# Graph attention on one core: steps of two edge slots instead of three, the carried sum taken by TensorE and copied back by ScalarE

## The chip, the cores and the metric

The kernel runs on 1 core of a Trainium2 chip. The metric is the device time in microseconds (us). The kernel before took 4021.01 us, the median of 3 runs (4016.24 to 4050.6). The profiled execution took 4017.71 us; its span in the trace is 4015.6 us.

## The reference, cut to what matters

There are 12500 nodes of 256 features, 8 heads of 32, and 200000 edges between random nodes. All is fp32.

```
q, k, v = (h @ W.T + b).reshape(N, 32, 8)       # for Wq, Wk, Wv; q * 32**-0.5
s = einsum('edh,edh->eh', q[row], k[col])       # one score per edge and head
e = exp(s - segment_max(s, row)[row])
attn = e / segment_sum(e, row)[row]
out = segment_sum(attn * v[col], row)
return layernorm(x + out @ Wo.T + bo)
```

## The kernel before, in words

A first part sorts the edges by node, counts the edges of every node (a histogram), orders the nodes by that count, and writes a table `kv_rows` to HBM with one row per node: its keys (256) and, for each head, its 32 values and a 1 (8 x 33 = 264). The 12500 nodes are cut into 98 tiles of 128, so that a partition holds one node, and nodes with nearly the same number of edges share a tile. A last part (`finish`) divides by the sum of weights, multiplies by Wo and normalises.

Between the two stands `one_round`, the main loop. A slot is one edge for each of the 128 nodes of a tile, and a tile has as many slots as its fullest node has edges. A step takes G = 3 slots of one tile. The number of steps, 598, is fixed when the program is built, as an upper bound. With these inputs, the sum over the tiles of the fullest node's edges divided by 3 and rounded up is 559; the other 39 steps are padding, which gather row 0 of the table for every slot and work on a 99th tile that nobody reads. For steps of two slots the same count gives 813 of 849, and 36 of padding. No node has more than 36 edges, so that one round of `C` slots is enough.

What a step does, with its engines and lines:

- ScalarE copies the step's node numbers into `idx` (`indices`, L973; it looks the place up in a table, by a register load).
- GpSimd starts one indirect DMA for each slot (`gather`, L931): 128 rows of 520 numbers into `kv`. SyncE loads the tile's 128 rows of q (`load_q`, L952). Both run up to U = 6 steps ahead.
- VectorE multiplies keys by q (`score`, L790), sums each head (`score_sum`, L797), looks tile and place of a later step up (`look_up`, L853), copies the tile's old maximum behind the scores (L802), adds the mask (L805), takes the new maximum (L812) and subtracts it (`differences`, L818).
- ScalarE takes exp of the differences (`weights`, L977), that of the old maximum too, which is the factor by which the old sum has to shrink.
- VectorE multiplies the values of the first G - 1 slots by their weights (`weigh`, L825), ScalarE those of the last slot, head by head, in 8 instructions (`weigh_last`, L987).
- TensorE sums the slots by multiplying each with the identity into one PSUM tile `sum_ps` (`total`, L1032 for the first slots, L1034 for the last).
- VectorE scales the tile's accumulator in SBUF, `acc`, by the shrink factor (`scale_acc`, L836) and adds `sum_ps` of the step before (`add_sum`, L844).

Each engine's order is written out by hand. VectorE works at three steps at once: in step k it sums the scores of k+1, weighs k, adds the sum of k-1, and multiplies for k+2. `prod` is a single buffer; `s`, `pv` and `sum_ps` have two. Every engine takes its instructions in order, and a wait on a semaphore stands before the instruction that needs it.

Of the kernel before, what the change touches and what calls it, by code (L numbers as in the profile page):

```python
# [12 lines left out]
P = 128  # L13
N, D, E = 12500, 256, 200000
HEADS = 8
HD = D // HEADS
# [22 lines left out]
G = 3  # L39
QR = 2 * R  # L40
BP = 65
C = 39
TAB = TILES + 1
U = 6
V = G - 1
B = 6
# [625 lines left out]
def one_round(nc, new_sem, kv_rows, edge_keys, q_perm, ident, ones, upper, node_id, start_f, tile_deg,  # L672
# [8 lines left out]
    with ExitStack() as ps:  # L681
# [3 lines left out]
        def pp(name, shape, dtype=F32):  # L685
# [12 lines left out]
        pv = sb("pv", [P, 2, G * VW])  # L698

        room = pv[:, :, :].rearrange("p b w -> p (b w)")  # L700
        step_f, past, tile_f = room[:, 0:STEPS], room[:, STEPS:2 * STEPS], kv[0:1, U - 1, :, :].rearrange("p g w -> p (g w)")[:, 0:STEPS]
        place_f = prod[0:1, :, :].rearrange("p g d -> p (g d)")[:, 0:STEPS]
# [11 lines left out]
        exp_made, pv_made, last_made, acc_scaled, summed, acc_added = (  # L714
            sem(x) for x in ("exp_made", "pv_made", "last_made", "acc_scaled", "summed", "acc_added"))
# [4 lines left out]
        with nc.Block() as block:  # L720

            @block.vector
            def _(dve):
# [76 lines left out]
                def mask_scores(k, b, col, tile):  # L800

                    dve.tensor_copy(s[:, b, G * HEADS:], runmax[:, bass.ds(tile * HEADS, HEADS)]).then_inc(old_copied, 1)  # L802
                    dve.wait_ge(scored, k + 1)
                    sv = s[:, b, 0:G * HEADS].rearrange("p (g h) -> p g h", h=HEADS)
                    dve.tensor_tensor(sv, sv, mflat[:, bass.ds(col, G)].unsqueeze(2).to_broadcast([P, G, HEADS]), ALU.add).then_inc(masked, 1)  # L805
# [43 lines left out]
                tile_r = [dve.alloc_register(f"tile_{b}") for b in range(3)]  # L849
                col_r = [dve.alloc_register(f"col_{b}") for b in range(3)]  # L850

                def look_up(k, c):
                    v = dve.value_load(step_tab[0:1, bass.ds(k, 1)], min_val=0, max_val=TAB * C * P - 1)  # L853
                    dve.reg_mov(tile_r[c], v & (P - 1))
                    dve.reg_mov(col_r[c], v >> PBITS)

                def step(k, j, turn, peel=False, last=False):

                    b, b1 = j % 2, (j + 1) % 2
                    score_sum(k + 1, b1, peeled=peel and j == 0)  # L860
                    weigh(k, j % U, b, peeled=peel and j < 2)

                    tile, tile1, col1 = (bounded(dve, tile_r[j % 3], TILES), bounded(dve, tile_r[(j + 1) % 3], TILES),
                                         bounded(dve, col_r[(j + 1) % 3], TAB * C - G))
                    before = None if peel and j == 0 else bounded(dve, tile_r[(j + 2) % 3], TILES)
                    look_up(k + 2, (j + 2) % 3)
# [14 lines left out]
                mask_scores(0, 0, col, tile)  # L881
# [12 lines left out]
                tile, before = bounded(dve, tile_r[k % 3], TILES), bounded(dve, tile_r[(k - 1) % 3], TILES)  # L894
                add_sum(k - 1, (k - 1) % 2, before)
                scale_acc(k, k % 2, tile)
                add_sum(k, k % 2, tile)
# [66 lines left out]
            def _(act):  # L964
# [14 lines left out]
                def weigh_last(k, j, turn, b, peeled=False):  # L979
# [5 lines left out]
                    for h in range(HEADS):  # L985
                        at_h = h * (HD + 1)
                        last = act.activation(pv[:, b, V * VW + at_h:V * VW + at_h + HD + 1], kv[:, j, V, D + at_h:D + at_h + HD + 1],  # L987
                                              ACT.Copy, scale=s[:, b, V * HEADS + h:V * HEADS + h + 1])
                    last.then_inc(last_made, 1)
# [6 lines left out]
                weigh_last(0, 0, 0, 0, peeled=True)  # L996
                for k in range(B):
                    indices(k + U, k % U, 1)
                    weights(k + 1, (k + 1) % 2)
                    weigh_last(k + 1, (k + 1) % U, (k + 1) // U, (k + 1) % 2, peeled=k == 0)  # L1000
                with act.Fori(1, LOOPS - 1) as kk:
                    for j in range(B):
                        k = kk * B + j
                        indices(k + U, j % U, kk * (B // U) + j // U + 1)
# [219 lines left out]
```

## Time and profile before

| | before |
|---|---|
| median of 3 runs | 4021.01 us |
| profiled execution | 4017.71 us |
| its span | 4015.6 us |
| VectorE busy | 80% |
| GpSimd busy | 61% |
| TensorE matmul busy | 55% |
| ScalarE busy | 37% |
| steps of the main loop | 598 |

The shares are means over the whole span. The main loop takes the stretch from 1268 us to 3716 us; in the 40 slices of the page VectorE stands at 9 tenths or more in nearly all of it. A row of a timeline has the start in us, the length in us, the engine, the line, the operation, what it writes and reads, how many instructions were merged, and in brackets how long the engine sat idle before and what released it.

### The profile page before, as it was taken

The numbers are of one execution on the slowest core, as the hardware profiler recorded it, in microseconds if no ns is written. First come the engines' busy times: TensorE is split into PE (matmuls) and PEld (weight loads), VectorE is DVE, ScalarE is ACT, GpSimd is POOL, SyncE is SP. The second block draws the span as 40 slices with busy tenths as digits, with TensorE's granted clock in tenths as the row PEclk, the third lists the DMA queues.
The fourth block names the chain that finished last, engine by engine and source line by source line (L and its number), as shares of the span: only waits on it lengthen the run. The fifth ranks groups of instructions, "written<-read, shape, count | busy, mean of one in ns | idle before, by whom it ended". The sixth has DMA issues, their size and how long they took to land. (4 is left out here: it accounts for less than half of the span.)

```text
span 4015.6 us, 59591 instructions
## 1 busy us (share of the span) xinstructions
PE 2227.2 (55%) x7109; PEld 1514.8 (38%) x7109; DVE 3211.0 (80%) x8164; ACT 1504.6 (37%) x6480; POOL 2447.6 (61%) x2365
## 2 busy tenths in 40 slices
PE   3999888653002555555555545555555555544776
PEld 3788775432001333333333333333333333323443
DVE  8554467799223999999999999999999999977776
ACT  0110002221001555555555555555555555534332
POOL 3221120003767777777777777777777777765677
PEclk9966568776555788778777787777877778766777
DMA  1211013226513788878887887888777788799222
GB/s 33 64 58 32 16 43 101 89 67 125 171 36 96 231 233 232 232 232 232 231 232 232 232 232 231 232 232 231 232 232 231 232 232 232 229 177 169 80 92 85
DMA packets 329217, 665.86 MB, mean 166 GB/s; under 512 B 63462, under 2 KB 191750, under 8 KB 329016
## 3 DMA queue, kind: packets, MB, share of 16 engines
q0 software_dynamic: 160768, 518.27, 46.4%
q1 hardware_dynamic: 168392, 146.96, 12.7%
q8 instruction: 20, 0.33, 0.0%
q14 instruction: 37, 0.30, 0.0%
HBM read 599.35 MB, written 65.86 MB: 166 GB/s over the span
## 5 line engine op out<-in xcount | busy, mean ns | idle before, releaser
L931 POOL DMA_INDIRECT kv<-kv_rows,idx x1794 | 1863.0, 1038 | 583.7 <-issue 538.5
L1032 PE MATMUL sum_ps<-pv,ident 128*128 128x264 f32 x2392 | 902.0, 512 | 1299.3 <-DVE pv L825 1299.3
L1032 PEld LDWEIGHTS sum_ps<-pv,ident 128*128 128x128 f32 x2392 | 511.3, 237 | 1712.1 <-DVE pv L825 1393.1
L987 ACT ACTIVATE pv<-kv,s 128x33 f32<-128x33 f32 x4784 | 1084.4, 309 | 53.9 <-ACT s L977 27.3
L790 DVE TENSOR_TENSOR prod<-kv,q 128x768 f32<-128x768 f32 x598 | 569.2, 952 | 59.7 <-DMA kv<-kv_rows,idx 59.6
L797 DVE TENSOR_REDUCE s<-prod 128x24 f32<-128x768 f32 x598 | 565.5, 946 | 0.0
L977 ACT ACTIVATE s<-s 128x32 f32<-128x32 f32 x598 | 137.0, 229 | 1126.1 <-DVE s L818 1126.1
L1034 PE MATMUL sum_ps<-pv,ident 128*128 128x264 f32 x1196 | 497.3, 508 | 0.0
L507 PE MATMUL hist_ps<-hot_lo,hot_hi 125*98 125x128 bf16 x1600 | 372.1, 409 | 121.7 <-DVE hot_hi L174 121.7
L825 DVE TENSOR_TENSOR pv<-kv,s 128x528 f32<-128x528 f32 x598 | 417.4, 698 | 0.3 <-ACT s L977 0.3
L507 PEld LDWEIGHTS hist_ps<-hot_lo,hot_hi 125*98 125x98 bf16 x1600 | 370.3, 259 | 123.2 <-issue 68.7
L492 POOL DMA_INDIRECT kv_st<-node_rows,node_id x98 | 102.8, 1049 | 464.4 <-issue 444.4
L472 POOL TENSOR_SCALAR hot_hi<-hi_b 125x320 bf16<-125x320 bf16 x140 | 149.7, 1072 | 377.8 <-PE hist_ps L507 356.7
L172 DVE TENSOR_SCALAR hot_lo<-lo_b 125x320 bf16<-125x320 bf16 x640 | 164.2, 334 | 206.5 <-PE hist_ps L507 206.5
L1034 PEld LDWEIGHTS sum_ps<-pv,ident 128*128 128x128 f32 x1196 | 296.6, 248 | 70.3 <-ACT pv L987 0.4
L844 DVE TENSOR_TENSOR acc<-acc,sum_ps 128x264 f32 x598 | 256.6, 429 | 22.2 <-PE sum_ps L1034 1.1
L575 ACT ACTIVATE kv_st<-kv_ps 128x256 f32<-128x256 f32 x98 | 37.6, 383 | 589.3 <-PE q_ps L519 589.3
L836 DVE TENSOR_TENSOR acc<-acc,s 128x264 f32 x598 | 255.0, 426 | 0.3
L518 PE MATMUL kv_ps<-w_sb,xt_sb 128*128 128x512 f32 x392 | 200.5, 636 | 0.0
L812 DVE TENSOR_REDUCE runmax<-s 128x32 f32 x598 | 123.7, 207 | 79.3
L973 ACT ACTIVATE idx<-cols 128x3 int32 x598 | 113.2, 189 | 139.0 <-DVE round_base L782 136.6
L1178 POOL DMA_INDIRECT x<-in_x_rows,node_id x98 | 112.7, 1150 | 56.9 <-issue 30.7
(164 smaller groups left out, 2450.5 us busy)
## 6 DMA issues: line engine op xcount, KB each, us to landing
q<-q_perm SPq DMA_DIRECT2D x598, 128.0 KB, 3.7
kv<-kv_rows,idx POOLq DMA_INDIRECT x1794, 4.0
kv_rows<-kv_st SPq DMA_DIRECT2D x98, 260.0 KB, 3.0
xt_sb<-in_xT SPq DMA_DIRECT2D x98, 128.0 KB, 3.2
node_rows<-q_st SPq DMA_DIRECT2D x98, 128.0 KB, 3.4
q_perm<-kv_st SPq DMA_DIRECT2D x98, 128.0 KB, 1.9
kv_st<-node_rows,node_id POOLq DMA_INDIRECT x98, 3.1
cols<-edge_keys,run_at POOLq DMA_INDIRECT x98, 2.5
```

The source lines that it names most:

```text
L172: dve.tensor_scalar(hot_lo[:, v, :], lo_b[:, c * CH:(c + 1) * CH], float(v), None, ALU.is_equal)
L507: last = pe.matmul(hist_ps[0:TILES, 0:P], hot_hi[:, :, e], hot_lo[:, :, e], start=c == 0 and e == 0, stop=c == CHUNKS - 1 and e == CH - 1)
L518: pe.matmul(ps[:, 0:b - a], xt_sb[:, j, kc, :], w_sb[:, kc, a:b], start=kc == 0, stop=False)
L790: dve.tensor_tensor(prod[:, :, :], kv[:, j, :, 0:D], q[:, j, :].unsqueeze(1).to_broadcast([P, G, D]), ALU.mult).then_inc(prod_made, 1)
L797: dve.tensor_reduce(s[:, b, 0:G * HEADS], prod[:, :, :].rearrange("p g (h d) -> p (g h) d", d=HD), AX.X, ALU.add).then_inc(scored, 1)
L825: dve.tensor_tensor(pv[:, b, 0:V * VW].rearrange("p (g h w) -> p g h w", g=V, w=HD + 1), kv[:, j, 0:V, D:KVW].rearrange("p g (h w) -> p g ...
L836: dve.tensor_tensor(at_tile, at_tile, s[:, b, G * HEADS:].unsqueeze(2).to_broadcast([P, HEADS, HD + 1]), ALU.mult).then_inc(acc_scaled, 1)
L844: dve.tensor_tensor(at_tile, at_tile, sum_ps[b][:, 0:VW], ALU.add).then_inc(acc_added, 1)
L931: pool.indirect_dma_start(out=kv[:, j, g, :], out_offset=None, in_=kv_rows, in_offset=bass.IndirectOffsetOnAxis(ap=idx[:, j, g:g + 1], axi ...
L987: last = act.activation(pv[:, b, V * VW + at_h:V * VW + at_h + HD + 1], kv[:, j, V, D + at_h:D + at_h + HD + 1], ACT.Copy, scale=s[:, b, V ...
L1032: pe.matmul(sum_ps[b][:, 0:VW], ident[:, :], pv[:, b, g * VW:(g + 1) * VW], start=g == 0, stop=False)
L1034: pe.matmul(sum_ps[b][:, 0:VW], ident[:, :], pv[:, b, V * VW:G * VW], start=False, stop=True).then_inc(summed, 1)
```

## The change

A step has two slots (G = 2), and there are 849 steps. `kv`, `q` and `idx` have U = 8 buffers instead of 6, the loops unroll B = 8 steps, and a tile may have C = 40 slots. VectorE weighs one slot and ScalarE the other.

The accumulator is no longer scaled in place. VectorE writes the scaled accumulator into a third part of `pv` (`carry`). TensorE adds it to the two slots by one more multiplication with the identity, so that `sum_ps` holds the new accumulator, and ScalarE copies it back to `acc` (`store`), after looking up the tile. The store of step k stands in ScalarE's order within `weigh_last` of step k+1, behind 3 of the 8 heads. The look-up of VectorE moves to the head of its step, the copy of the old maximum to before `weigh`, and `indices` of ScalarE from before `weights` to behind `weigh_last`. The tables of the steps are built in the room of `kv`.

```diff
-G = 3
+G = 2
-C = 39
+C = 40
-U = 6
+U = 8
-B = 6
+BEFORE_STORE = 3
+B = 8
...
-        pv = sb("pv", [P, 2, G * VW])
+        pv = sb("pv", [P, 2, (G + 1) * VW])
...
-                def scale_acc(k, b, tile, first=False):
-
+                def carry(k, b, tile, first=False):
                     if not first:
-                        dve.wait_ge(acc_added, k)
-                    dve.wait_ge(exp_made, k + 1)
-                    at_tile = acc[:, bass.ds(tile * VW, VW)].rearrange("p (h w) -> p h w", w=HD + 1)
-                    dve.tensor_tensor(at_tile, at_tile,
-                                      s[:, b, G * HEADS:].unsqueeze(2).to_broadcast([P, HEADS, HD + 1]), ALU.mult).then_inc(acc_scaled, 1)
-
-                def add_sum(k, b, tile):
-
-                    dve.wait_ge(acc_scaled, k + 1)
-                    dve.wait_ge(summed, k + 1)
-                    at_tile = acc[:, bass.ds(tile * VW, VW)]
-                    dve.tensor_tensor(at_tile, at_tile, sum_ps[b][:, 0:VW], ALU.add).then_inc(acc_added, 1)
+                        dve.wait_ge(acc_stored, k)
+                    dve.tensor_tensor(pv[:, b, G * VW:].rearrange("p (h w) -> p h w", w=HD + 1),
+                                      acc[:, bass.ds(tile * VW, VW)].rearrange("p (h w) -> p h w", w=HD + 1),
+                                      s[:, b, G * HEADS:].unsqueeze(2).to_broadcast([P, HEADS, HD + 1]), ALU.mult).then_inc(carry_made, 1)
...
                     b, b1 = j % 2, (j + 1) % 2
+                    tile, tile1, col1 = bounded(dve, tile_r[b], TILES), bounded(dve, tile_r[b1], TILES), bounded(dve, col_r[b1], TAB * C - G)
+                    look_up(k + 2, b)
                     score_sum(k + 1, b1, peeled=peel and j == 0)
+                    old_maximum(k + 1, b1, tile1)
                     weigh(k, j % U, b, peeled=peel and j < 2)
...
-                    mask_scores(k + 1, b1, col1, tile1)
+                    mask_scores(k + 1, b1, col1)
+                    carry(k, b, tile, first=peel and j == 0)
                     maxima(k + 1, b1, tile1)
-                    if before is not None:
-                        add_sum(k - 1, b1, before)
                     if not last:
                         score(k + 2, (j + 2) % U, turn + (j + 2) // U)
-                    scale_acc(k, b, tile, first=peel and j == 0)
                     differences(k + 1, b1, tile1)
...
+                def weigh_heads(j, b, heads):
+
+                    for h in heads:
...
+                    weigh_heads(j, b, range(0, BEFORE_STORE))
+                    if stored:
+                        store(k - 1, 1 - b)
+                    weigh_heads(j, b, range(BEFORE_STORE, HEADS)).then_inc(last_made, 1)
+
+                def store(k, b):
+
+                    v = act.value_load(step_tab[0:1, bass.ds(k, 1)], min_val=0, max_val=TAB * C * P - 1)
+                    tile = bounded(act, v & (P - 1), TILES)
+                    act.wait_ge(summed, k + 1)
+                    act.activation(acc[:, bass.ds(tile * VW, VW)], sum_ps[b][:, 0:VW], ACT.Copy).then_inc(acc_stored, 1)
...
                     pe.wait_ge(last_made, k + 1)
-                    pe.matmul(sum_ps[b][:, 0:VW], ident[:, :], pv[:, b, V * VW:G * VW], start=False, stop=True).then_inc(summed, 1)
...
+                    pe.matmul(sum_ps[b][:, 0:VW], ident[:, :], pv[:, b, V * VW:G * VW], start=False, stop=False)
+                    pe.wait_ge(carry_made, k + 1)
+                    pe.matmul(sum_ps[b][:, 0:VW], ident[:, :], pv[:, b, G * VW:], start=False, stop=True).then_inc(summed, 1)
```

VectorE's order at the turn from one step to the next, before. L844 adds the sum, L790 is the product, L836 scales the accumulator, L818 the differences, L797 the sum of the scores, L825 the weighing, and the rows after it are the look-up:

```order
L844 ISA [waits summed,acc_scaled]
L844 TENSOR_TENSOR acc<-acc,sum_ps 128x264
L790 TENSOR_TENSOR prod<-kv,q 128x768 [waits q_in0,kv_in0]
L836 ISA [waits exp_made,acc_added]
L836 TENSOR_TENSOR acc<-acc,s 128x264
L818 TENSOR_TENSOR s<-s,runmax 128x32 [waits max_made]
L797 TENSOR_REDUCE s<-prod 128x24 [waits last_made,prod_made]
L825 TENSOR_TENSOR pv<-kv,s 128x528 [waits summed,exp_made]
L609 ISA
L853 TENSOR_LOAD step_tab
L853 ISA x2
```

The same place now. L837 is the carry, L816 the maximum, L791 the product, L822 the differences, and L798 the sum of the scores:

```order
L837 ISA [waits acc_stored]
L837 TENSOR_TENSOR pv<-acc,s 128x264
L816 TENSOR_REDUCE runmax<-s 128x8 [waits masked,old_copied,tab_ready]
L791 TENSOR_TENSOR prod<-kv,q 128x512 [waits q_in3,kv_in3]
L822 TENSOR_TENSOR s<-s,runmax 128x24 [waits max_made]
L610 ISA
L848 TENSOR_LOAD step_tab
L848 ISA x2
L849 REGISTER_ALU
L849 ISA
L798 TENSOR_REDUCE s<-prod 128x16 [waits last_made,prod_made]
```

The carry, with its wait on ScalarE's store, now stands ahead of maximum, product and differences, and the look-up stands between the differences and the next sum of scores.

ScalarE's order for one step now. L966 is the exp, L972 a head, L992 the store, L958 the look-up of the indices:

```order
L966 ACTIVATE s<-s 128x24 [waits diffs_made]
L979 ISA [waits exp_made]
L972 ACTIVATE pv<-kv,s 128x33 [waits summed,kv_in1]
L972 ACTIVATE pv<-kv,s 128x33 x2
L989 ISA
L989 TENSOR_LOAD step_tab
L989 ISA x2
L991 REGISTER_ALU
L992 REGISTER_ALU [waits summed]
L992 ISA
L992 ACTIVATE acc<-sum_ps 128x264
L972 ACTIVATE pv<-kv,s 128x33 x5
```

The register load and the store stand behind three heads and ahead of the five that TensorE's second multiplication waits for.

## Rows read from the trace of the kernel before

**Rows 1.** The page: busy time, share and instructions of each engine.

```profile
PE 2227.2 (55%) x7109; PEld 1514.8 (38%) x7109; DVE 3211.0 (80%) x8164; ACT 1504.6 (37%) x6480; POOL 2447.6 (61%) x2365
```

**Rows 2.** Stretches: stretch, length, PE, PEld, DVE, ACT, POOL, clock, DMA share, GB/s.

```profile
2000.00:2500.00 500.00, 264.68 (x750) 166.01 (x750) 467.94 (x1124) 266.17 (x1246) 385.99 (x375) 0.79 0.80 232
3510.00:3710.00 200.00, 98.71 (x226) 60.49 (x225) 144.65 (x338) 79.97 (x373) 126.34 (x115) 0.65 0.95 176
```

**Rows 3.** GpSimd's gathers in 2000 to 3000 us: busy, mean ns, idle before.

```profile
L931 POOL DMA_INDIRECT kv<-kv_rows,idx x749 | 773.2, 1032 | 228.3 <-issue 228.3
```

**Rows 4.** Timeline of one step amid the main loop.

```profile
2400.24 1.81 ACT L987 ACTIVATE pv<-kv,s 128x33 f32<-128x33 f32 x8
2400.72 0.70 DVE L825 TENSOR_TENSOR pv<-kv,s 128x528 f32<-128x528 f32 x1
2401.47 1.16 PE L1032 MATMUL sum_ps<-pv,ident 128*128 128x264 f32 x4 [2.36 <-DVE pv L825]
2401.50 0.17 DVE L802 COPY s<-runmax 128x8 f32 x1
2401.64 0.18 DVE L805 TENSOR_TENSOR s<-s,mask 128x24 f32<-128x24 f32 x1
2401.96 0.21 DVE L812 TENSOR_REDUCE runmax<-s 128x32 f32 x1
2401.96 0.19 ACT L973 ACTIVATE idx<-cols 128x3 int32 x1
2402.17 0.43 DVE L844 TENSOR_TENSOR acc<-acc,sum_ps 128x264 f32 x1
2402.47 0.61 PE L1034 MATMUL sum_ps<-pv,ident 128*128 128x264 f32 x2
2402.52 0.95 DVE L790 TENSOR_TENSOR prod<-kv,q 128x768 f32<-128x768 f32 x1
2403.39 0.43 DVE L836 TENSOR_TENSOR acc<-acc,s 128x264 f32 x1
2403.73 0.19 DVE L818 TENSOR_TENSOR s<-s,runmax 128x32 f32<-128x32 f32 x1
2403.84 0.95 DVE L797 TENSOR_REDUCE s<-prod 128x24 f32<-128x768 f32 x1
2403.95 0.23 ACT L977 ACTIVATE s<-s 128x32 f32<-128x32 f32 x1 [1.81 <-DVE s L818]
```

**Rows 5.** Timeline: first product, and the last one of the main loop.

```profile
1267.84 0.96 DVE L790 TENSOR_TENSOR prod<-kv,q 128x768 f32<-128x768 f32 x1 [8.16 <-DMA kv<-kv_rows,idx]
3715.31 0.95 DVE L790 TENSOR_TENSOR prod<-kv,q 128x768 f32<-128x768 f32 x1
```

**Rows 6.** DMA queues in the padding, 3520 to 3700 us: packets, MB, share.

```profile
q0 software_dynamic: 8280, 27.55, 86.1%
q1 hardware_dynamic: 4752, 4.33, 10.2%
```

**Rows 7.** Timeline of the last step, where nothing covers the waits.

```profile
3719.92 0.23 ACT L977 ACTIVATE s<-s 128x32 f32<-128x32 f32 x1 [1.10 <-DVE s L818]
3720.18 1.81 ACT L987 ACTIVATE pv<-kv,s 128x33 f32<-128x33 f32 x8
3722.04 0.71 PE L1034 MATMUL sum_ps<-pv,ident 128*128 128x264 f32 x2
3722.86 0.43 DVE L844 TENSOR_TENSOR acc<-acc,sum_ps 128x264 f32 x1 [1.06 <-PE sum_ps L1034]
```

**Rows 8.** Timeline: ScalarE copies out of PSUM, one behind the other.

```profile
629.31 0.38 ACT L575 ACTIVATE kv_st<-kv_ps 128x256 f32<-128x256 f32 x1 [104.21 <-PE q_ps L519]
629.59 0.38 ACT L576 ACTIVATE kv_st<-kv_ps 128x256 f32<-128x256 f32 x1
```

**Rows 9.** Timeline: the second index copy, with nothing ahead of it.

```profile
1261.18 0.21 ACT L973 ACTIVATE idx<-cols 128x3 int32 x1 [0.48 <-issue]
```

**Rows 10.** Timeline: TensorE's first slots of a step, at the lower clock.

```profile
2413.63 2.13 PE L1032 MATMUL sum_ps<-pv,ident 128*128 128x264 f32 x4 [1.96 <-DVE pv L825]
```

More of the change, by code:

```diff
@@ L713, in one_round @@
             sem(x) for x in ("prod_made", "scored", "old_copied", "masked", "max_made", "diffs_made"))
-        exp_made, pv_made, last_made, acc_scaled, summed, acc_added = (
-            sem(x) for x in ("exp_made", "pv_made", "last_made", "acc_scaled", "summed", "acc_added"))
+        exp_made, pv_made, last_made, carry_made, summed, acc_stored = (
+            sem(x) for x in ("exp_made", "pv_made", "last_made", "carry_made", "summed", "acc_stored"))
         CUT = 512
@@ L846, in _, with look_up @@
                 dve.wait_ge(tab_ready, 1)
                 dve.wait_ge(runs_ready, 1)
-                tile_r = [dve.alloc_register(f"tile_{b}") for b in range(3)]
-                col_r = [dve.alloc_register(f"col_{b}") for b in range(3)]
-                def look_up(k, c):
+                tile_r = [dve.alloc_register(f"tile_{b}") for b in range(2)]
+                col_r = [dve.alloc_register(f"col_{b}") for b in range(2)]
+                def look_up(k, b):
                     v = dve.value_load(step_tab[0:1, bass.ds(k, 1)], min_val=0, max_val=TAB * C * P - 1)
-                    dve.reg_mov(tile_r[c], v & (P - 1))
-                    dve.reg_mov(col_r[c], v >> PBITS)
+                    dve.reg_mov(tile_r[b], v & (P - 1))
+                    dve.reg_mov(col_r[b], v >> PBITS)
@@ L893, in _ @@
                 weigh(k, k % U, k % 2)
[L894 to L897, printed above, removed]
+                carry(k, k % 2, bounded(dve, tile_r[k % 2], TILES))
                 for r in tile_r + col_r:
@@ L977, in weights, with weigh_last @@
                     act.activation(s[:, b, :], s[:, b, :], ACT.Exp).then_inc(exp_made, 1)
-                def weigh_last(k, j, turn, b, peeled=False):
+                def weigh_heads(j, b, heads):
+                    for h in heads:
+                        at_h = h * (HD + 1)
+                        last = act.activation(pv[:, b, V * VW + at_h:V * VW + at_h + HD + 1], kv[:, j, V, D + at_h:D + at_h + HD + 1],
+                                              ACT.Copy, scale=s[:, b, V * HEADS + h:V * HEADS + h + 1])
+                    return last
+                def weigh_last(k, j, turn, b, stored=True, peeled=False):
                     act.wait_ge(exp_made, k + 1)
@@ L984, in weigh_last @@
                         act.wait_ge(summed, k - 1)
[L985 to L989, printed above, removed]
+                    weigh_heads(j, b, range(0, BEFORE_STORE))
[7 more added lines that the diff above has]
+                    act.activation(acc[:, bass.ds(tile * VW, VW)], sum_ps[b][:, 0:VW], ACT.Copy).then_inc(acc_stored, 1)
                 act.wait_ge(tab_ready, 1)
@@ L1003, in _ @@
                         k = kk * B + j
-                        indices(k + U, j % U, kk * (B // U) + j // U + 1)
                         weights(k + 1, (j + 1) % 2)
                         weigh_last(k + 1, (j + 1) % U, kk * (B // U) + (j + 1) // U, (j + 1) % 2)
+                        indices(k + U, j % U, kk * (B // U) + j // U + 1)
                 for k in range((LOOPS - 1) * B, STEPS - 1):
+                    weights(k + 1, (k + 1) % 2)
+                    weigh_last(k + 1, (k + 1) % U, (k + 1) // U, (k + 1) % 2)
                     if k + U < STEPS:
                         indices(k + U, k % U, (k + U) // U)
-                    weights(k + 1, (k + 1) % 2)
-                    weigh_last(k + 1, (k + 1) % U, (k + 1) // U, (k + 1) % 2)
+                store(STEPS - 1, (STEPS - 1) % 2)
             @block.tensor
@@ L1033, in total @@
                     pe.wait_ge(last_made, k + 1)
-                    pe.matmul(sum_ps[b][:, 0:VW], ident[:, :], pv[:, b, V * VW:G * VW], start=False, stop=True).then_inc(summed, 1)
-                for j in range(B):
-                    total(j, j % 2, peeled=j < 2)
-                with pe.Fori(1, LOOPS) as kk:
+                    pe.matmul(sum_ps[b][:, 0:VW], ident[:, :], pv[:, b, V * VW:G * VW], start=False, stop=False)
+                    pe.wait_ge(carry_made, k + 1)
+                    pe.matmul(sum_ps[b][:, 0:VW], ident[:, :], pv[:, b, G * VW:], start=False, stop=True).then_inc(summed, 1)
+                with pe.Fori(0, LOOPS) as kk:
                     for j in range(B):
```

24 lines of the change are left out of this document (10 added, 14 removed).

## The prediction

> **What bounds the kernel now.** I read the page first, then stretches, then one step as a timeline, then the two places where nothing covers a wait. The page gives VectorE 80% of the span [rows 1]. The stretch amid the main loop gives it 468 of 500 us, and 1124 instructions at 9 a step are 124.9 steps, so 4.00 us a step [rows 2]. The timeline of one step shows why: nine VectorE instructions from L825 at 2400.72 to the end of L797 at 2404.79, none with a wait, 4.07 us, less the 0.08 by which such instructions overlap (L790 ends at 2403.47, L836 starts at 2403.39): 3.99 [rows 4]. GpSimd is close: a gather is 1.03 us and 0.30 us of issue before it, three of them 4.01 us [rows 3]. ScalarE idles 1.81 us in a step [rows 4], and DMA moves 232 GB/s at a share of 0.80 [rows 2]. So VectorE sets 559 real steps.
>
> The main loop takes 3715.31 - 1267.84 = 2447.5 us [rows 5]. 559 x 4.00 are 2236 us; the other 211 are 39 padding steps (338 instructions at 9 a step are 37.6 in 200 us, 5.3 us each) and a slow start, with DMA in the padding at a share of 0.95 but only 176 GB/s [rows 2]: there all gathers read one row, and DMA sets the pace. Outside the loop stand 4017.7 - 2447.5 = 1570 us, which the change leaves (one gather less ahead of the first product is 1.3 us; 40 instead of 39 slots in the masks are below 1 us).
>
> **VectorE's part gets shorter.** By starts, 264 elements cost 0.34 us (L836) and 768 cost 0.87 (L790) [rows 4], so 512 cost 0.60. A new step: sum of scores 0.60, copy 0.14, weigh 0.34, mask 0.14, carry 0.34, maximum 0.21, product 0.60, differences 0.11: 2.48 us. 813 of them are 2016 us against 2236: the adds and the wider shapes that go save VectorE 220 us. GpSimd's two gathers need at most 2.67 us a step [rows 3]. A gather is 128 rows of 2080 bytes, 266 KB, a load of q 131 KB; DMA moves 663 KB a step where it moved 929 in 4.00; at 3 us a step that is 221 GB/s, under today's 232, so I cost the 251 more loads of q at nothing: DMA idles a fifth of the time, SyncE only starts them, and they run up to 8 steps ahead. Were that cover gone, they would cost as in the padding, half a us a step. The loop pays only if a step stays under (2447.5 - 135) / 813 = 2.84 us, the 135 being the padding below.
>
> **The cycle through ScalarE and VectorE.** The carry waits for the store of the step before, and behind the carry on VectorE stand maximum, product and differences; exp waits for these, the heads for exp, and the next store stands behind three heads. By pieces: store 0.39 (a 256-element copy out of PSUM takes 0.38 [rows 8]); to the carry 0.10 (TensorE's end at 3722.75 to the add at 3722.86, with the same kind of register instruction between, is 0.11 [rows 7]); carry 0.34; maximum 0.21; product 0.60; differences to exp 0.22; exp to the first head 0.26 [rows 4, 7]; three heads of 0.214 each ((1.81 - 0.31) / 7, with 0.31 for the last), 0.64. Sum 2.76 us. That is if the store's register load is ready when the third head has started. Bare, a look-up and its copy take 0.48 + 0.21 us [rows 9]; begun when exp is done, with three heads and two more register instructions to issue, the store would start some 0.95 us after the first head could: 3.07 us. Covered by more, it costs nothing: at 2401.96 the index copy has no gap behind eight heads [rows 4]. Three heads are less than half of that, so I take 2.95, nearer the bare end.
>
> The Trainium skill (DMA: Bandwidth & Descriptors, Latency and other measured facts) gives a register load a floor of about 600 ns; the bare pitch of 0.69 us with the copy agrees in size [rows 9]. By the page's figure alone this cycle would be about 3.0 us.
>
> **The cycle through TensorE.** This one is new. The last five heads of a step come behind the store of the step before; TensorE's second multiplication waits for them, the third (the carry) comes behind it, and the next store waits for both. From the store's start: next instruction after 0.28 [rows 8]; four heads 0.86, the last one's length 0.31; to TensorE 0.05 (heads end at 3721.99, matmul at 3722.04 [rows 7]); two passes with nothing ahead 0.71 [rows 7] and two more at 0.275 ((1.16 - 0.61) / 2 [rows 4]), 1.26; to the waiting engine 0.11 and another register instruction 0.05. Sum 2.92 us at the higher clock. With the closest pitches only (four passes 1.16, waits of 0.05) it would be 2.74. At the lower clock four passes take 2.13 us instead of 1.16 [rows 10, 4], and the cycle is 3.89. I take 2.92 for it.
>
> The clock granted is 0.79 in the main loop: 0.42 of the time stands at 1.2 GHz, the rest at 2.4. In the padding, with the same matmuls in 5.3 us steps, it is 0.65 [rows 2]. So denser work kept it higher, and the new step has the same six passes in 3 us instead of 4. I take one step in ten at the lower clock, which adds 0.10 us a step; ends: none, and 0.42 (0.41 us).
>
> The Trainium skill (TensorE: Matmul & The Clock Gate, Part 1: The HAM clock gate) says that the low clock is the default and that activity releases it. The two stretches agree in direction; by that rule without reserve the 0.10 would be nothing.
>
> **The look-up on VectorE.** Today 1.29 us pass from the end of exp (0.03 before the heads, 2400.21) to L802, which comes behind the look-up, and it is 0.08 us late behind L825 [rows 4]. Now the look-up begins once the differences are issued, about 0.2 us into the product, and has only product and differences above it. Taking 0.6 to 1.1 us for it, the next sum of scores starts 0.8 to 1.3 after the product's start (0.82 anyway: product 0.69 and 0.14 until its result can be read, as from L805's end to L812). Then 0.60 + 0.14 + 0.34 + 0.14 to the carry, 0.34 + 0.21 to the next product: 2.6 to 3.07 us. It runs beside the carry's wait, so it adds nothing unless it is the longest; I take 2.95.
>
> **The sum.** Three cycles lie between 2.9 and 3.0 us. I take the longest by my values, 2.95, and 0.10 for the clock: 3.05 us. 813 x 3.05 = 2480 us. Padding: of 5.3 us, gathers hold 86.1 of 96.3 parts and q 10.2 [rows 6], so 1.58 us for a gather and 0.56 for q, 3.7 us for two and q; 36 steps 135 us. In all 1570 + 2480 + 135 = **4185 us**, against the profiled 4017.7, which is 0.1% below the median of the runs. So 4% slower.
>
> **Rivals.** *The clock stays as it is* (0.42 of the steps at 1.2 GHz): 3.36 us a step, 4437 us. For it: it oscillates now, and the multiplications come in two bursts. Against: the padding's trend. *Register loads stand bare*: ScalarE's exp 0.26, eight heads 1.72, store 0.28, index copy 0.19 and two bare waits of 0.48 make 3.41 us if neither is covered, 3.2 if VectorE's or one of ScalarE's is; I price it at 3.2, 4307 us. Against it: the index copy is covered now. *All waits close to their shortest* (the other side): the store's load is covered by three heads and the TensorE cycle runs at its 2.74, so that steps take 2.75 us: 1570 + 2236 + 135 = 3941 us. For it: the ends of matmuls are modelled, and the last step alone shows exposed waits. It decides from below 2.79 us. *Little change*: a step of 2.80 to 2.88, 3980 to 4050 us.
>
> **Chances.** A measurement of this kernel tells about 1% from no change (4061 and 3981). Forecast (2.9 to 3.15 us, 4063 to 4265 us) 0.57; clock 0.15; bare loads 0.11; shortest waits 0.10; little change 0.07. So faster 0.10, within 1% 0.07, slower 0.83. The range leaves out the shortest waits and a part of the clock's case: 4030 to 4430 us.
>
> **What would show it.** In the changed profile: VectorE idle before the carry (L837), released by ScalarE's store; ScalarE idle before the store (L992), released by TensorE's last multiplication (my second cycle), or by issue (the register load); VectorE's busy share down to about 0.8 in the main loop; GpSimd waiting 0.3 to 0.5 us once a step; a clock above 0.85. A step at 2.75 with no idle before the store would prove the cycles mis-sized. VectorE idle before L798 by issue would put the look-up first. I would be wrong altogether if VectorE showed no waits and steps near 2.6 us.

## The result and the profile after

The changed kernel takes 4120.3 us, the median of 4 runs (4116.9 to 4120.5), against 4022.4 us before: a ratio of 1.0227, with a 95% interval of 1.0179 to 1.0276. It is slower by 98 us, where 4185 us was forecast. The profiled execution took 4120.48 us, its span is 4118.6 us. In all ratios a few longer executions are left out as slow ones, among them one of 5250.6 us in run 2 and some of the kernel before in the jobs of the experiments (up to 4186.7 us).

These are the page's busy times of the changed kernel, to be read beside [rows 1]: VectorE fell from 80% to 72%, ScalarE rose from 37% to 57%, TensorE from 55% to 62%. No engine is at its limit by this view.

```profile
PE 2547.3 (62%) x8615; PEld 1551.0 (38%) x8615; DVE 2947.2 (72%) x9574; ACT 2359.1 (57%) x9839; POOL 2362.5 (57%) x2269
```

Two stretches of the changed kernel answer to [rows 2], amid the main loop and in the padding (stretch, length, PE, PEld, DVE, ACT, POOL, clock, DMA share, GB/s):

```profile
2000.00:2500.00 500.00, 314.17 (x1006) 164.77 (x1004) 389.53 (x1337) 420.08 (x1840) 348.50 (x334) 0.99 0.77 222
3700.00:3810.00 110.00, 71.96 (x183) 36.97 (x182) 75.09 (x247) 76.83 (x337) 63.33 (x61) 0.80 0.99 182
```

A step now has 8 VectorE instructions, so 1337 are 167 steps, 2.99 us each, where 4.00 stood. The granted clock rose from 0.79 to 0.99. In the padding 247 instructions are 30.9 steps in 110 us, 3.6 us each where 5.3 stood.

One step of the changed kernel as a timeline, beside [rows 4] (rows of GpSimd, the loads of weights, the copy L803, the first passes L1034 and the index copy L962 left out):

```profile
2401.20 0.22 ACT L966 ACTIVATE s<-s 128x24 f32<-128x24 f32 x1 [0.25 <-DVE s L822]
2401.45 0.75 ACT L972 ACTIVATE pv<-kv,s 128x33 f32<-128x33 f32 x3
2401.46 0.61 PE L1038 MATMUL sum_ps<-pv,ident 128*128 128x264 f32 x2
2401.74 0.69 DVE L798 TENSOR_REDUCE s<-prod 128x16 f32<-128x512 f32 x1 [0.58 <-issue]
2402.27 0.39 ACT L992 ACTIVATE acc<-sum_ps 128x264 f32 x1
2402.41 0.43 DVE L829 TENSOR_TENSOR pv<-kv,s 128x264 f32<-128x264 f32 x1
2402.55 1.16 ACT L972 ACTIVATE pv<-kv,s 128x33 f32<-128x33 f32 x5
2402.76 0.17 DVE L809 TENSOR_TENSOR s<-s,mask 128x16 f32<-128x16 f32 x1
2402.84 0.43 DVE L837 TENSOR_TENSOR pv<-acc,s 128x264 f32<-128x264 f32 x1
2403.19 0.17 DVE L816 TENSOR_REDUCE runmax<-s 128x24 f32 x1
2403.28 0.68 DVE L791 TENSOR_TENSOR prod<-kv,q 128x512 f32<-128x512 f32 x1
2403.77 0.71 PE L1036 MATMUL sum_ps<-pv,ident 128*128 128x264 f32 x2 [0.16 <-ACT pv L972]
2403.88 0.18 DVE L822 TENSOR_TENSOR s<-s,runmax 128x24 f32<-128x24 f32 x1
2404.32 0.61 PE L1038 MATMUL sum_ps<-pv,ident 128*128 128x264 f32 x2
2404.62 0.69 DVE L798 TENSOR_REDUCE s<-prod 128x16 f32<-128x512 f32 x1 [0.57 <-issue]
2405.13 0.39 ACT L992 ACTIVATE acc<-sum_ps 128x264 f32 x1
```

The sum of scores starts at 2401.74 and at 2404.62, 2.88 us apart, and before each VectorE is idle by issue, for 0.58 and 0.57 us: that is the look-up, which now stands there. It stands behind the wait of the differences for the maximum, and 1.26 us pass from the maximum's end at 2403.36 to the sum at 2404.62. The other two cycles are closed as well. The five heads end at 2403.71, TensorE starts 0.06 later, ends its four passes at 2404.93, and the store follows 0.20 later at 2405.13, 2.86 us after the one before. And the three heads ahead of the store at 2402.27 start 0.82 us before it, though three heads take 0.64 by their starts: the register load stands there, or the wait for TensorE, whose passes ended at 2402.07. These rows cannot tell the two apart; run 5 does.

The waits of 2000 to 3000 us say the same in total (engine, what it waited for, us, times, longest). The 335 times are the steps:

```profile
DVE s L798 <- issue: 210.0, 335, 1.1
DVE pv L837 <- ACT acc L992: 8.3, 35, 0.8
ACT acc L992 <- PE sum_ps L1038: 4.6, 5, 1.0
```

**Where the time went**, by products in the two traces. Before, the loop of 2447 us [rows 5] is 559 real steps in 2247 us (4.02 us each) and 201 us of padding. After, it lasts from 1265.0 to 3818.4, 2553 us: 813 real steps in 2430 us (2.99 us each) and 123 us of padding. The real steps cost 184 us more, the padding 78 us less, and outside the loop 3 us fewer stand than before.

**What the mean step is made of.** Away from the loop's turn a step takes 2.88 us. Two steps in every eight take 3.36 and 3.13 us: that is the turn, 0.73 us, or 0.09 us a step. And 16 of the 813 real steps take 0.5 to 0.96 us more than the others at their place in the loop, 13 us in all or 0.02 us a step. In them the four passes run at the lower clock, wholly or in part, and the store waits for TensorE, as in the five waits of the list above:

```profile
2331.51 1.25 PE L1036 MATMUL sum_ps<-pv,ident 128*128 128x264 f32 x2 [0.38 <-ACT pv L972]
2332.55 1.09 PE L1038 MATMUL sum_ps<-pv,ident 128*128 128x264 f32 x2
2333.84 0.39 ACT L992 ACTIVATE acc<-sum_ps 128x264 f32 x1 [1.02 <-PE sum_ps L1038]
2334.37 0.43 DVE L837 TENSOR_TENSOR pv<-acc,s 128x264 f32<-128x264 f32 x1 [0.83 <-ACT acc L992]
```

The four passes take 2.13 us instead of 1.16, and the step from the product at 2331.01 to the one at 2334.81 is 3.80 us.

### The profile page after: what moved, and what is told of

Same layout as the page of the kernel before. It is cut to its first block and busy times, and to the rows that moved or that the text cites. A ratio compares the mean times of both kernels' runs of the same rounds, so it can differ in the third digit from the quotient of the medians.

```text
span 4118.6 us, 78055 instructions
## 1 busy us (share of the span) xinstructions
PE 2547.3 (62%) x8615; PEld 1551.0 (38%) x8615; DVE 2947.2 (72%) x9574; ACT 2359.1 (57%) x9839; POOL 2362.5 (57%) x2269
## 5 line engine op out<-in xcount | busy, mean ns | idle before, releaser
L972 ACT ACTIVATE pv<-kv,s 128x33 f32<-128x33 f32 x6792 | 1621.0, 312 | 56.3 <-ACT s L966 35.5
L1034 PE MATMUL sum_ps<-pv,ident 128*128 128x264 f32 x1698 | 620.1, 448 | 929.6 <-DVE pv L829 929.4
L798 DVE TENSOR_REDUCE s<-prod 128x16 f32<-128x512 f32 x849 | 582.3, 686 | 524.8 <-issue 524.7
L1034 PEld LDWEIGHTS sum_ps<-pv,ident 128*128 128x128 f32 x1698 | 258.5, 192 | 1290.1 <-DVE pv L829 1290.0
L1036 PE MATMUL sum_ps<-pv,ident 128*128 128x264 f32 x1698 | 617.1, 446 | 152.6 <-ACT pv L972 121.0
L791 DVE TENSOR_TENSOR prod<-kv,q 128x512 f32<-128x512 f32 x849 | 580.0, 683 | 23.1 <-DMA kv<-kv_rows,idx 23.0
L1038 PE MATMUL sum_ps<-pv,ident 128*128 128x264 f32 x1698 | 530.1, 395 | 0.0
L837 DVE TENSOR_TENSOR pv<-acc,s 128x264 f32<-128x264 f32 x849 | 361.9, 426 | 33.0 <-ACT acc L992 29.0
L992 ACT ACTIVATE acc<-sum_ps 128x264 f32 x849 | 331.2, 390 | 82.6 <-PE sum_ps L1038 21.4
L829 DVE TENSOR_TENSOR pv<-kv,s 128x264 f32<-128x264 f32 x849 | 361.9, 426 | 0.3 <-ACT s L966 0.3
L966 ACT ACTIVATE s<-s 128x24 f32<-128x24 f32 x849 | 189.1, 223 | 291.4 <-DVE s L822 291.4
L962 ACT ACTIVATE idx<-cols 128x2 int32 x849 | 161.6, 190 | 140.0 <-DVE round_base L783 136.7
L803 DVE COPY s<-runmax 128x8 f32 x849 | 217.3, 256 | 0.0
```

What stands on the lines that cost most here:

```text
L791: dve.tensor_tensor(prod[:, :, :], kv[:, j, :, 0:D], q[:, j, :].unsqueeze(1).to_broadcast([P, G, D]), ALU.mult).then_inc(prod_made, 1)
L798: dve.tensor_reduce(s[:, b, 0:G * HEADS], prod[:, :, :].rearrange("p g (h d) -> p (g h) d", d=HD), AX.X, ALU.add).then_inc(scored, 1)
L829: dve.tensor_tensor(pv[:, b, 0:V * VW].rearrange("p (g h w) -> p g h w", g=V, w=HD + 1), kv[:, j, 0:V, D:KVW].rearrange("p g (h w) -> p g ...
L837: dve.tensor_tensor(pv[:, b, G * VW:].rearrange("p (h w) -> p h w", w=HD + 1), acc[:, bass.ds(tile * VW, VW)].rearrange("p (h w) -> p h w" ...
L992: act.activation(acc[:, bass.ds(tile * VW, VW)], sum_ps[b][:, 0:VW], ACT.Copy).then_inc(acc_stored, 1)
L1034: pe.matmul(sum_ps[b][:, 0:VW], ident[:, :], pv[:, b, g * VW:(g + 1) * VW], start=g == 0, stop=False)
```

## The experiments

All are timed against the kernel before, in the same job. The figure for one step away from the loop's turn is the distance between two products in the profile.

**1. VectorE's look-up back behind the weighing.**

```diff
-                    look_up(k + 2, b)
                     score_sum(k + 1, b1, peeled=peel and j == 0)
                     old_maximum(k + 1, b1, tile1)
                     weigh(k, j % U, b, peeled=peel and j < 2)
+                    look_up(k + 2, b)
```

> The changed kernel with VectorE's look-up moved from the head of its step to behind the weighing, where the kernel before had it. In the changed kernel every step shows 0.57 us of idle by issue before the sum of scores (L798) and a step of 2.87 us, 2.98 with the turns of the loop. Theory A (the look-up's register work, about 1.15 us after the differences are issued, sets the step): behind the weighing it has sum of scores, copy and weighing above it, but can begin only after exp is done, so the idle by issue moves behind the weighing and shrinks to 0.3 to 0.4 us; steps of 2.75 to 2.82 and 4000 to 4070 us. Theory B (the look-up runs beside TensorE's cycle of multiplication, store and five heads, which is itself 2.85 us): no gain, 4110 to 4125 us.

4061.8 us, ratio 1.0110 (1.0094 to 1.0126): 58 us less than the changed kernel. The idle by issue moved to the mask and shrank to 0.38:

```profile
2402.29 1.16 ACT L972 ACTIVATE pv<-kv,s 128x33 f32<-128x33 f32 x5
2402.32 0.18 DVE L809 TENSOR_TENSOR s<-s,mask 128x16 f32<-128x16 f32 x1 [0.38 <-issue]
2404.86 0.39 ACT L992 ACTIVATE acc<-sum_ps 128x264 f32 x1
```

But the step fell only from 2.88 to 2.86 us. Theory A had the time about right for the wrong reason. The mean step went from 2.99 to 2.92 us, and about half of that is the loop's turn: two steps of 3.36 and 3.13 us in every eight became 3.04 and 3.13. The rest is 0.02 us of the step itself and 0.02 of steps at the lower clock, of which there is one now. Away from the turn something else holds 2.86 us.

**2. VectorE without the register load.**

```diff
-                    v = dve.value_load(step_tab[0:1, bass.ds(k, 1)], min_val=0, max_val=TAB * C * P - 1)
-                    dve.reg_mov(tile_r[b], v & (P - 1))
-                    dve.reg_mov(col_r[b], v >> PBITS)
+                    dve.reg_mov(tile_r[b], k >> 4)
+                    dve.reg_mov(col_r[b], k + k)
```

> The changed kernel without VectorE's register load: VectorE takes tile and place from the step's number (k >> 4 and 2k) instead of the table, so it reads and scales other tiles than the step's own; all instructions and waits but the load stay. Theory A alone (look-up, nothing else close): the 0.57 us before L798 go to the 0.14 that the product needs, and GpSimd's two gathers of 1.34 us are next, steps of 2.67 us, about 3870 us. Theory B (the cycle store, five heads, second and third multiplication, by the changed trace 0.28 + 1.16 + 0.06 + 1.16 + 0.10 to 0.2, is right behind): steps of 2.76 to 2.85, 3940 to 4020 us, with ScalarE now idle before the store by TensorE in most steps.

4064.1 us, ratio 1.0108 (1.0090 to 1.0126), the same as run 1, and the same 2.86 us. VectorE has nothing to wait for now but the store, and waits for it. ScalarE does not stand idle before the store, as theory B expected; the three heads fill the time.

```profile
2404.78 0.43 DVE L837 TENSOR_TENSOR pv<-acc,s 128x264 f32<-128x264 f32 x1 [0.51 <-ACT acc L991]
```

So the look-up was one of several limits of the same length, neither theory as it was put: theory B had its cycle at the right length, but its time did not allow for the turns.

**3. Three slots with the new way of carrying the sum.** The changed kernel with G = 3, C = 39, U = 6, B = 6.

> The new way of carrying the sum alone: steps of three slots as before (G 3, 6 buffers, 6 steps unrolled, 39 slots), carry on VectorE, third multiplication on TensorE, store on ScalarE. VectorE loses its add of 0.35 us a step; its part would be 3.1 us and some 0.25 of bare look-up, so GpSimd's three gathers (3.9 to 4.0 us) set the step. If the new path's waits are harmless with longer steps: steps of 3.92 to 4.0 us, 3975 to 4020 us. If the cycle through TensorE and ScalarE is what costs, it would show here too, with one more weighing but the same cycle of about 2.9 us, so no loss either; above 4040 us would speak against both.

4181.0 us, ratio 1.0399 (1.0381 to 1.0416). A miss: neither case allowed 4181. The profile shows VectorE waiting for gathered rows and GpSimd's gathers longer than 1.03 us:

```profile
2401.37 0.96 DVE L791 TENSOR_TENSOR prod<-kv,q 128x768 f32<-128x768 f32 x1 [0.74 <-DMA kv<-kv_rows,idx]
2401.89 1.32 POOL L920 DMA_INDIRECT kv<-kv_rows,idx  x1 [0.30 <-issue]
```

```profile
L920 POOL DMA_INDIRECT kv<-kv_rows,idx x694 | 788.9, 1137 | 211.6 <-issue 190.8 <-ACT idx L962 19.2 <-DVE pv L829 1.2
```

The product ends at 2402.33 and the gather that started beside it at 2403.21, 0.88 later. The same distance of 0.87 to 0.88 us stands in the other runs where a gather starts while a product is running (run 1: product to 2400.81, gather from 2400.43 to 2401.68). The weighing does the same, here from run 8, where it ends at 2402.80 and the gather at 2403.67:

```profile
2402.10 0.70 DVE L829 TENSOR_TENSOR pv<-kv,s 128x528 f32<-128x528 f32 x1
2402.33 1.34 POOL L922 DMA_INDIRECT kv<-kv_rows,idx  x1 [0.30 <-issue]
```

A gather at whose start none of product, weighing and carry is running takes 1.00 us (never above 1.02 between 1400 and 3400 us in eight of the traces), even when one of them starts a moment later, and so does one that starts beside the sum of the scores, which reads one tile. Before, all gathers kept a rhythm with VectorE: the one in three that started beside the product did so near its end and took 1.06 us. Now VectorE is faster than GpSimd and waits for rows, the rhythm is lost, product, weighing and carry fall anywhere beside the gathers, and the mean gather is longer: 3 x (1.137 + 0.305) = 4.33 us a step instead of 4.01 [rows 3]. GpSimd never stands for more than the 0.30 us that precede every gather, so it is the engine that is full.

The Trainium skill (SBUF — State Buffer, SBUF: two separate sides) says that a VectorE instruction with two SBUF inputs and a GpSimd operation that reads SBUF exclude each other. The gathers agree with it: they are held by product, weighing and carry, which read two tiles, and not by the sum of the scores. In the other direction nothing is seen: the weighing at 2400.72 in the kernel before, 0.05 us after a gather's start, took its usual 0.70 us [rows 4].

**4. Two slots with the old sum.** The kernel before with G = 2, C = 40 and its tables built in `kv`.

> The narrow step alone: two slots, 849 steps, 40 slots of room, but the old accumulator (scaled and added to in place by VectorE, look-up behind the weighing), 6 buffers and 6 steps unrolled. VectorE's instructions sum to about 3.1 us by their starts. Theory A (the look-up cannot start before exp is done and takes about 1.2 us from there, with less above it than at three slots): 0.4 to 0.6 us of idle by issue before L802, steps of 3.5 to 3.7 us, 4550 to 4720 us. If the look-up stays covered: steps of 3.15, about 4280 us.

4712.0 us, ratio 1.1723 (1.1704 to 1.1742), theory A's upper end. The look-up begins when exp is done and L802 comes 1.29 us after exp's end, the same as at three slots (exp ends at 2401.98, L802 starts at 2403.27), but with less above it:

```profile
2402.24 0.42 DVE L825 TENSOR_TENSOR pv<-kv,s 128x264 f32<-128x264 f32 x1
2403.27 0.24 DVE L802 COPY s<-runmax 128x8 f32 x1 [0.60 <-issue]
2403.72 0.18 DVE L812 TENSOR_REDUCE runmax<-s 128x24 f32 x1
```

The step is 3.68 us. So two slots alone would cost 690 us, and the new way of carrying the sum, with the look-up at the head of the step, gives back 592 of them; in this figure stand the deeper buffers and the eight unrolled steps too, which were not tried alone.

**5. TensorE takes the carry second and ScalarE's slot last**, on top of run 1.

```diff
+                    pe.wait_ge(carry_made, k + 1)
+                    pe.matmul(sum_ps[b][:, 0:VW], ident[:, :], pv[:, b, G * VW:], start=False, stop=False)
                     pe.wait_ge(last_made, k + 1)
-                    pe.matmul(sum_ps[b][:, 0:VW], ident[:, :], pv[:, b, V * VW:G * VW], start=False, stop=False)
-                    pe.wait_ge(carry_made, k + 1)
-                    pe.matmul(sum_ps[b][:, 0:VW], ident[:, :], pv[:, b, G * VW:], start=False, stop=True).then_inc(summed, 1)
+                    pe.matmul(sum_ps[b][:, 0:VW], ident[:, :], pv[:, b, V * VW:G * VW], start=False, stop=True).then_inc(summed, 1)
```

> Look-up behind the weighing (as in the run before this, 4062 us, steps of 2.86 us), and TensorE takes the carry second and ScalarE's slot last, so that only two passes instead of four stand between the fifth head and the store. Theory C (TensorE's cycle sets 2.86): the cycle loses 0.55 us, the next one is the carry's (store 0.55 to the carry, 0.35, 0.09, 0.60, 0.21, 0.25, three heads 0.64 and up to 0.17 of bare register load: 2.69 to 2.86), so steps of 2.70 to 2.80, 3930 to 4015 us. Theory D (the carry's cycle with the store's register load sets 2.86 as well): 4055 to 4065 us. Theory E (GpSimd: a gather cannot end sooner than 0.87 us after a product ends, and when GpSimd is the slowest it meets the product in every step, as with three slots, where its gather rose from 1.03 to 1.14 us): two gathers of 1.14 + 0.30 are 2.87, no gain either, but VectorE would show waits on kv.

4051.1 us, ratio 1.0060 (1.0028 to 1.0091), 11 us less than run 1, steps of 2.84 to 2.86 us. TensorE is now done at 2401.93, 0.64 us before the store, and the store still comes 0.81 us after the first head at 2401.76:

```profile
2401.30 0.63 PE L1038 MATMUL sum_ps<-pv,ident 128*128 128x264 f32 x2
2401.76 0.75 ACT L972 ACTIVATE pv<-kv,s 128x33 f32<-128x33 f32 x3
2402.57 0.39 ACT L992 ACTIVATE acc<-sum_ps 128x264 f32 x1
```

Three heads take 0.64 by their starts, so the register load holds the store by 0.17 us. The carry follows the store, not the mask:

```profile
2402.89 0.17 DVE L809 TENSOR_TENSOR s<-s,mask 128x16 f32<-128x16 f32 x1 [0.38 <-issue]
2403.12 0.43 DVE L837 TENSOR_TENSOR pv<-acc,s 128x264 f32<-128x264 f32 x1
```

Theory D: the carry's cycle holds 2.85 us as well. Theory E is out as far as VectorE shows no wait on `kv`.

**6. TensorE's order alone**, the same edit on the changed kernel with nothing else.

> The changed kernel with nothing but TensorE's order turned round (carry second, ScalarE's slot last). If VectorE's bare look-up alone sets the changed kernel's step (2.87 us; the look-up needs about 1.25 us from the end of the maximum), nothing moves: 4110 to 4125 us. If TensorE's cycle is what sets it and the idle by issue only fills the time, it falls by as much as in the run before: 4000 to 4060 us.

4106.9 us, ratio 1.0198 (1.0158 to 1.0237), 13 us under the changed kernel; the step stays at 2.88 us, with 210.3 us of issue before L798 in 1000 us, as before. The look-up alone holds the step. The 13 us are the steps at the lower clock: there are 2 with 0.8 us more in all, where the changed kernel has 16 with 13 us. The expectation's range was missed by 3 us.

**7. The store behind two heads instead of three**, on top of run 1.

```diff
-BEFORE_STORE = 3
+BEFORE_STORE = 2
```

> Look-up behind the weighing, and the store behind two heads instead of three. TensorE's cycle then has six heads behind the store and grows by 0.21 us; the carry's cycle shrinks by 0.21, as far as the register load lets it. Theory C (TensorE's cycle sets the step): steps of 3.07 us, 4220 to 4240 us. Theory D (the carry's cycle sets it): 3900 to 4062 us.

4192.5 us, ratio 1.0408 (1.0367 to 1.0448), and a step of 3.07 us, to the hundredth theory C's. The time is 28 us under its range, since the turns no longer show (3.07 to 3.10 in all steps). ScalarE waits for TensorE's sum before the store in each of the 325 steps of the stretch:

```profile
ACT acc L992 <- PE sum_ps L1038: 147.4, 325, 0.5
DVE pv L837 <- ACT acc L992: 79.0, 324, 0.3
```

One head more in TensorE's cycle adds one head's 0.21 us to run 1's step. So this cycle is 2.86 us long at three heads; it was there and closed.

**8. Three slots, but two gathers.** Run 3 without the gather of the middle slot, whose buffer stays zero.

```diff
-                    for g in range(G):
+                    for g in (0, G - 1):
```

> Three slots with the new way of carrying the sum, but GpSimd leaves out the gather of the middle slot (its buffer is zero), so VectorE, ScalarE and TensorE do the same work and GpSimd and DMA a third less. The run with all three took 4181 us, with steps of 4.2 to 4.3. Theory E (GpSimd became the slowest and its gathers, delayed by the products, set 4.3 us): VectorE's own 3.4 us set the step, 3600 to 3750 us. Theory F (the new waits of carry and store cost it): 4100 us or more.

3722.0 us, ratio 0.9242 (0.9206 to 0.9277), in theory E's range, with steps of 3.45 us (3.60 on the mean with the turns). With a third less of gathers the waits for rows are nearly gone (2.7 us in 1000 where run 3 has 160.4):

```profile
DVE prod L791 <- DMA kv<-kv_rows,idx: 2.7, 4, 0.9
```

So in run 3 the gathers, not carry and store, cost the time. The run takes away DMA traffic together with GpSimd's work; of the two, GpSimd is seen to be full in run 3's rows, while DMA's share there was 0.76, below the 0.80 of the kernel before [rows 2].

**9. The store's look-up ahead of the exp**, on top of run 5. The load and the register move stand before `weights`, and `store` only uses the register.

```diff
+                def old_tile(k):
+                    v = act.value_load(step_tab[0:1, bass.ds(k, 1)], min_val=0, max_val=TAB * C * P - 1)
+                    act.reg_mov(tile_a, v & (P - 1))
...
-                    v = act.value_load(step_tab[0:1, bass.ds(k, 1)], min_val=0, max_val=TAB * C * P - 1)
-                    tile = bounded(act, v & (P - 1), TILES)
+                    tile = bounded(act, tile_a, TILES)
...
+                        old_tile(k)
                         weights(k + 1, (j + 1) % 2)
```

> As the run with TensorE's carry second and the look-up behind the weighing (4051 us, steps of 2.85 us), and ScalarE looks the store's tile up ahead of the exp instead of between third head and store, where its sequencer waits for the differences anyway. In that run the store starts 0.81 us after the first head, where three heads take 0.64, and TensorE has been done for 0.64 us. Theory D (carry's cycle, store held by its bare register load): the cycle loses up to 0.17 us, then VectorE's own 2.72 us (its look-up is bare by 0.38) are next: steps of 2.70 to 2.75, 3950 to 3975 us, under the kernel before. If GpSimd's two gathers with their delay (1.25 + 0.30 + 1.00 + 0.30 = 2.85) set it: 4045 to 4055 us, unchanged.

3976.6 us, ratio 0.9892 (0.9863 to 0.9921): 75 us less than run 5, and 1.1% faster than the kernel before. The store starts 0.65 us after the first head, no later than the heads make it; the two long steps of a turn are now 2.90 and 2.83:

```profile
2401.01 0.22 ACT L966 ACTIVATE s<-s 128x24 f32<-128x24 f32 x1 [0.24 <-DVE s L822]
2401.26 0.75 ACT L972 ACTIVATE pv<-kv,s 128x33 f32<-128x33 f32 x3
2401.91 0.37 ACT L995 ACTIVATE acc<-sum_ps 128x264 f32 x1
2402.40 0.17 DVE L809 TENSOR_TENSOR s<-s,mask 128x16 f32<-128x16 f32 x1 [0.39 <-issue]
2402.55 0.43 DVE L837 TENSOR_TENSOR pv<-acc,s 128x264 f32<-128x264 f32 x1
```

The step is 2.79 us, above the 2.70 to 2.75 expected. What holds it now is a fourth cycle, from the exp through the look-up to the next exp: exp's end to the mask 1.17, mask to carry 0.15, carry to differences 1.04, differences to exp 0.21, exp 0.22, in sum 2.79. The carry comes 0.15 us behind the mask, where 0.08 stood in the changed kernel; that is the 0.07 us that the expectation lacked. The store has ended 0.27 us before the carry and no longer holds it. GpSimd's two gathers fill this step too (1.19 + 0.30 + 1.00 + 0.30), but the first ends 0.87 us after the product and shortens with the step, and VectorE waited for rows only once between 1300 and 3500 us, for 0.3 us; so GpSimd keeps pace and does not set it. Away from the loop's turns 0.06 us a step was gained, on the mean 0.09 (2.90 to 2.81), since a turn now costs 0.14 us where it cost 0.47.

**10. Sixteen steps unrolled**, run 9 with B = 16.

> The same with 16 steps unrolled instead of 8, so half as many turns of the loop. A turn costs 0.44 us in the run before (two steps of 3.04 and 3.12 instead of 2.86), 105 turns 46 us: 20 to 25 us less than with 8, whatever sets the step. If the longer loop body costs instruction loading instead: no gain or a loss.

4268.4 us, ratio 1.062 (1.0588 to 1.0652): 292 us more, not 20 less. Steps are 2.79 us as before, but two in every sixteen take 5.6 to 6.9 and 3.4 to 5.7 us, and three more 3.0 to 3.3. The instruction queue of the page moves 4.89 MB instead of 0.34, first run 10, then run 9:

```profile
q14 instruction: 597, 4.89, 0.4%
```

```profile
q14 instruction: 41, 0.34, 0.0%
```

Between 2000 and 2500 us, amid the loop, run 10 has 109 of these packets, and run 9 none:

```profile
q14 instruction: 109, 0.89, 0.6%
```

That is about 11 packets for each turn of 51 us: some of the loop's instructions are loaded again in every turn, which with eight steps they are not. That the long steps wait for these packets is argued from their falling once a turn; no row names the packets as what ended a wait.

## Why the prediction was right, point by point

**The bound before and VectorE's saving.** The new VectorE instructions cost by their starts what was worked out (product 0.60, carry 0.35), but the short ones less: copy 0.07, mask 0.08, maximum 0.09, where 0.14, 0.14 and 0.21 were taken. VectorE's part is 2.25 us a step, not 2.48. The saving is real, and goes into waits.

**Three cycles near 2.9 us.** The forecast took 2.95 for the carry's cycle, 2.92 for TensorE's and 2.95 for the look-up's. Measured: about 2.85 (run 5 leaves it as the limit, run 9 frees it), 2.86 (run 7 adds one head and finds 3.07) and 2.88 (run 6). All three are there, and the longest is the look-up's. TensorE's was 0.06 too long: its four passes take 1.16 us from a standing start, not 1.26, while the step from its end to the store takes 0.20, not 0.16. Of the signs named, the look-up's came (VectorE idle by issue before L798 in every step); the idle of VectorE before the carry, 8.3 us in 1000, and of ScalarE before the store, 4.6 us, came in a few steps only.

**The look-up's length, in part luck.** The forecast put the next sum of scores 0.8 to 1.3 us behind the product's start; it comes after 1.34 (2403.28 to 2404.62), longer than any value taken. 2.95 us leave 1.18 for it. From the sum to the next product the forecast took 1.77; measured are 1.54 (2401.74 to 2403.28), for the short instructions above. The two errors cancel but for 0.07 us.

**The register loads.** The store's load is bare by 0.17 us, which run 9 took away. On VectorE 1.29 us pass from the end of exp to the instruction behind the look-up, in the kernel before and in run 4 alike, and 1.26 from the maximum's end in the changed kernel. The Trainium skill (DMA: Bandwidth & Descriptors, Latency and other measured facts) gives a register load a floor of about 600 ns. The bare pitch of 0.69 us with its copy agrees in size [rows 9]; that figure is of the load alone, and VectorE's look-up with its register instructions takes twice as long.

**The clock.** The term of 0.10 us a step was mis-sized: it cost 0.02. The granted clock is 0.99, and 16 steps in 813 met the lower one, not one in ten. A step that meets it was priced at 3.89 us, and takes up to 3.83 away from the turns. The Trainium skill (TensorE: Matmul & The Clock Gate, Part 1: The HAM clock gate) says that activity releases the clock, and the trace agrees in direction, with 0.99 where 0.79 stood. The rival that kept the clock as it was is ruled out.

**The turns of the loop.** The forecast left them out beside the longest cycle. They cost 0.09 us a step. In the turn's first long step VectorE's idle by issue before the sum of scores is 1.04 us instead of 0.57:

```profile
2107.71 0.69 DVE L798 TENSOR_REDUCE s<-prod 128x16 f32<-128x512 f32 x1 [1.04 <-issue]
```

A turn costs 0.73 us here, 0.45 in run 1, 0.14 in run 9, and next to nothing in run 7, where TensorE's cycle holds the step. So it is dear where register instructions stand on the cycle that holds the step; that they are the loop's own is argued, not shown.

**The sum, luck in part.** 3.05 us a step were forecast and 2.99 came: 2.88 for the longest cycle instead of 2.95, 0.09 for turns that had no term, 0.02 for the clock instead of 0.10. The missing term and the one too large nearly cancel. The cycle of 2.88 us alone would have given 1567 + 2341 + 123 = 4031 us, which is the forecast's rival of little change and lies 1 us inside the range. The mechanism was right, and the time lies inside the forecast's own bounds with the help of the turns.

**The padding.** 123 us, where 135 were forecast by the shares of gathers and q.

**The rivals.** Bare loads at 3.2 us: they are bare, by 0.57 and 0.17 us, but side by side with the other waits and not in sum. Shortest waits at 2.75 us: no cycle is that short, the shortest found is 2.79 (and the forecast's closest pitches for TensorE's cycle add up to 2.71, not 2.74: 0.28 + 1.17 + 0.05 + 1.16 + 0.05). What the range had no case for is GpSimd's gather growing when VectorE waits for rows; it does not decide here, and it does at three slots (run 3).

## What to carry to other kernels

Work that is moved off the busiest engine has to be priced as the cycle it closes, from one step's result back to the same instruction of the next step, with its register loads and hand-overs; here three cycles of 2.85 to 2.88 us stood where VectorE's instructions take 2.25. When several such cycles are nearly equal, relieving one gains next to nothing away from the turns (0.02 us a step in run 1, 11 us in all in run 5) until all are relieved (75 us with the last). A register load cost nothing here where its sequencer was already ahead of the engine (the index copy) or stood waiting (run 9); behind a wait it was a term of its own. The turn of an unrolled loop wants a term too: 0.14 to 0.73 us a turn, by the cycle that holds the step.

## What the runs showed of the hardware

- A gather on GpSimd takes 1.00 us. One that starts while a VectorE instruction with two SBUF inputs is running (product, weighing, carry) ends 0.87 to 0.88 us after that instruction, if that is later: it took up to 1.8 us in run 3. One that has started before it, or starts beside the sum of the scores, with one input, takes 1.00 us.
- An unrolled loop of 16 steps moves 597 instruction packets instead of 41, about 11 in every turn, and takes 292 us more than one of 8.
- The granted clock was 0.65 with six passes in 5.3 us, 0.79 with six in 4.0 and 0.99 with six in 2.99 us; with four in 3.68 us it was 0.50, all of it at 1.2 GHz (run 4). Passes per us alone do not order it: with eight passes in 3.60 us it was 0.96 (run 8), with six in 3.07 us 1.00 (run 7).
- A step that met the lower clock in the changed kernel took up to 3.83 us away from the turns instead of 2.88, as four passes took 2.13 us instead of 1.16.
